# Attention of a macaron block on one core: values in batches of eight, masks in pairs at a batch's end, row maxima transposed at its start

## The chip, the cores and the metric

One core of a Trainium2 chip runs the whole program. Times are device microseconds (us) of one execution; the kernel before took 3117.17 us as the median of three runs (3116.67 to 3117.39). Engines are called PE (TensorE, the matmuls), DVE (VectorE), ACT (ScalarE), POOL (GpSimd) and SP (SyncE, which issues the transfers).

## What is computed

A block of 2048 tokens of 512 features: a feed-forward part, attention, and the same feed-forward part again. The change touches the attention alone, with 16 heads of 32 features:

```python
qkv = jnp.einsum('bsd,ed->bse', x, w_qkv) + b_qkv
scores = jnp.einsum('bhqd,bhkd->bhqk', q, k) / math.sqrt(Hd)
scores = scores + causal[None, None]          # -inf above the diagonal
attn = jax.nn.softmax(scores, axis=-1)
out = jnp.einsum('bhqk,bhkd->bhqd', attn, v)
```

The weights are scaled up, so that scores are large and each row's maximum has to be taken off before the exponential.

## The kernel before

Three stages run in the attention: `project_in` (line 788) makes queries, keys and values, `attention` (line 1125) works through the heads, `project_out` (line 1330) multiplies with the output weights. The change is in `attention`, in the class `Heads` (line 622) that serves it, and in the share of head 0 that `project_in` does at its end.

**Two passes over the scores.** A head's scores are computed twice on PE. The first time, queries stand on the output partitions: 40 chunks a head (`CHUNKS`, `max_chunk`, line 705) of up to 512 columns, of which DVE takes the row maximum (`take_max`, line 729; chunks on the diagonal are masked in the same instruction). When the last chunk of one of the four blocks of 512 queries is reduced, `split_max` (line 748) joins the maxima and splits them in two parts; PE transposes these in `rows` (line 719, four small matmuls with 2 columns of weights), and ACT copies the two rows under the head's queries (`store_rows`, line 761). The second time, keys stand on the output partitions: 40 tiles a head (`TILES`, `scores`, line 1196) of 128 keys by up to 512 queries, with the maximum subtracted by the two extra rows. A tile on the diagonal (16 of 40) gets a second, small bf16 matmul (line 1213, 128 columns) that adds the mask. ACT takes the exponential (`exps`, line 1273), and PE multiplies the result with the values (`with_values`, line 1217): 33 columns of weights, the values and a column of ones whose product is the softmax's sum. `TILES` alternates between two lanes, which write partitions 0 and 64 on, so that two products run side by side. `take_out` (line 1281) copies the output banks, twice a head.

**Banks.** PSUM has 8 banks: 3 for scores, 3 for chunks and transposed rows (`MAX_BANKS`), 2 for outputs. PE may write score tile u when the exponential of u - 3 is done, and an item of the maxima (`ITEMS`) when the item three before is taken out.

**The order.** It is written out by hand. In slot t of 40 of a head (`head`, line 1232), PE issues the score tile t + 4, the chunks of the next head that belong to slot t (one, in slots 0, 9, 18 and 27 two, in the last four none), and, in slots 17, 28, 35 and 39, the transposed rows of blocks 3, 2, 1 and 0 of the next head. After every fourth slot come four products with the values. So there are ten batches of products a head. Two lines set the distances:

```python
BATCH = 4
AHEAD = 4
```

Each engine works through its own list in order, so a wait holds up all that stands behind it on the engine. The last head has no next one, so it has no chunks, and ACT converts the output weights (line 1306) just before it. For head 0, the chunks and rows are spread over the last steps of `project_in` (`head_items_after`, line 778); the last step has nine of the 44 items, rows 1 and rows 0 as its last.

Of the kernel before, what the change touches and what calls it, by code (L numbers as in the profile page):

```python
# [8 lines left out]
F32 = mybir.dt.float32  # L9
# [585 lines left out]
SCORE_BANKS = 3  # L595
BATCH = 4
AHEAD = 4
RING = AHEAD + BATCH


ROWS_AFTER = 4


def chunks_of_slot(t):

    return [m for m in range(SLOTS) if m * (SLOTS - ROWS_AFTER) // SLOTS == t]


MAXED_AT = {[t for t in range(SLOTS) if LAST_CHUNK[b] in chunks_of_slot(t)][0]: b for b in BLOCKS}
ROWS_AT = {t + ROWS_AFTER: b for t, b in MAXED_AT.items()}  # L610

ITEMS = [item for t in range(SLOTS)
         for item in [("chunk", m) for m in chunks_of_slot(t)] + ([("rows", ROWS_AT[t])] if t in ROWS_AT else [])]
MAX_BANKS = 3
DIAGONAL = [m for m in range(SLOTS) if CHUNKS[m][2] == CHUNKS[m][0]]


def max_bank_of(s, item):
    return (len(ITEMS) * s + ITEMS.index(item)) % MAX_BANKS


class Heads:
# [49 lines left out]
    def add_slot(self, nc, ctx):  # L672
        i = len(self.queries)
        self.queries.append(ctx.enter_context(nc.sbuf_tensor(f"queries{i}", [self.ROWS, TOKENS], F32R)))
        self.keys.append(ctx.enter_context(nc.sbuf_tensor(f"keys{i}", [self.ROWS, TOKENS], F32R)))
        self.values.append(ctx.enter_context(nc.sbuf_tensor(f"values{i}", [P, TT, VCOLS], F32)))
        ctx.enter_context(nc.sbuf_tensor(f"values_pad{i}", [P, TT, HD], F32))

# [15 lines left out]
    def wait_for_max_bank(self, pe, hp, s, item):  # L694

        before = len(ITEMS) * s + ITEMS.index(item) - MAX_BANKS
        if before < 0:
            return
        (kind, j), s = ITEMS[before % len(ITEMS)], before // len(ITEMS)
# [18 lines left out]

    def rows(self, pe, hp, s, b):

        pe.wait_ge(self.max_parts_ready, 12 * hp + (4 * s + RANK[b] + 1))
        self.wait_for_max_bank(pe, hp, s, ("rows", b))
# [55 lines left out]
def head_items_after(ep, s, tb):  # L778
# [3 lines left out]
    if i < 0:  # L782
        return []
    end = len(ITEMS) if i == steps - 1 else len(ITEMS) * (i + 1) // (steps + LEFT_TO_LAST)
    return ITEMS[len(ITEMS) * i // (steps + LEFT_TO_LAST):end]

# [338 lines left out]
def attention(nc, bank, o_heads, sums, inverses, w_out, b_out, heads, o):  # L1125
    with ExitStack() as ctx:
# [67 lines left out]
        def _(pe):  # L1194

            def scores(hp, s, t, first=False):

                b, kt = TILES[t]
                i = s % 3
                if t in FIRST_OF_BLOCK:  # L1200
                    pe.wait_ge(heads.rows_ready, 12 * hp + (4 * s + RANK[b] + 1))
                    if s == 2 and t == 0:
                        pe.wait_ge(heads.constants_ready, 9)
                if not (first and t < SCORE_BANKS):
                    pe.wait_ge(probs_ready, 120 * hp + (SLOTS * s + t - SCORE_BANKS + 1))
                q0 = max(b * TB, kt * P)
                width = (b + 1) * TB - q0
                out = score_bank[(SLOTS * s + t) % SCORE_BANKS]
                last = pe.matmul(out[:, 0:width], keys[i][0:ROWS, cols(kt, P)],  # L1209
                                 queries[i][0:ROWS, q0:q0 + width], start=True, stop=(kt < 4 * b),  # L1210
                                 skip_group_check=True)
                if kt >= 4 * b:
                    last = pe.matmul(out[:, 0:P], heads.ident_b[:], heads.key_mask_b[:],
                                     start=False, stop=True, skip_group_check=True)
                last.then_inc(scores_ready, 1)

            def with_values(hp, s, t):
# [4 lines left out]
                if t % BATCH == 0:  # L1222
# [3 lines left out]
                last = pe.matmul(out_bank[BANK_OF[b]][row:row + VCOLS, off:TB], values[i][:, kt, :],  # L1226
                                 probs[:, t % RING, 0:TB - off], start=(t in FIRST_OF_BLOCK),
                                 stop=(t in LAST_OF_BLOCK), skip_group_check=True)
# [3 lines left out]
            def head(hp, s, has_next):  # L1232
                for t in range(SLOTS):
                    if t + AHEAD < SLOTS:
                        scores(hp, s, t + AHEAD)
                    elif has_next:
                        scores(hp, s + 1, t + AHEAD - SLOTS)
                    if has_next:
                        for m in chunks_of_slot(t):
                            heads.max_chunk(pe, hp, s + 1, m)  # L1240
                        if t in ROWS_AT:
                            heads.rows(pe, hp, s + 1, ROWS_AT[t])
                    if t % BATCH == BATCH - 1:
                        for u in range(t + 1 - BATCH, t + 1):
                            with_values(hp, s, u)

            for t in range(AHEAD):
                scores(0, 0, t, first=True)
            with pe.Fori(0, HEADS // 3) as hp:
# [5 lines left out]
        def _(dve):  # L1255
            def head(hp, s):
                for t in range(SLOTS):
                    for m in chunks_of_slot(t):
                        heads.take_max(dve, hp, s + 1, m)
                    if t in MAXED_AT:  # L1260
                        heads.split_max(dve, hp, s + 1, MAXED_AT[t])

# [9 lines left out]
        def _(act):  # L1272
            def exps(hp, s, t):
                b, kt = TILES[t]
                width = TB - max(0, kt * P - b * TB)
                act.wait_ge(scores_ready, 120 * hp + (SLOTS * s + t + 1))
                source = score_bank[(SLOTS * s + t) % SCORE_BANKS][:, 0:width]
                act.activation(probs[:, t % RING, 0:width], source, ACT.Exp, scale=SM_SCALE)\  # L1278
                   .then_inc(probs_ready, 1)

# [6 lines left out]
            def head(hp, s, has_next):  # L1287
                for t in range(SLOTS):
                    if t + AHEAD < SLOTS:
                        exps(hp, s, t + AHEAD)  # L1290
                    elif has_next:
                        exps(hp, s + 1, t + AHEAD - SLOTS)
                    if has_next and t in ROWS_AT:
                        heads.store_rows(act, hp, s + 1, ROWS_AT[t])
                    if t % BATCH == BATCH - 1:
# [3 lines left out]

            for t in range(AHEAD):  # L1300
                exps(0, 0, t)
            with act.Fori(0, HEADS // 3) as hp:
# [233 lines left out]
```

## Time and profile before

| | |
|---|---|
| median of three runs | 3117.17 us |
| the profiled execution, its own time | 3117.0 us |
| its span | 3115.2 us |
| lies around the span | 1.8 us |
| first product with values of head 0, of head 1 | 1296.24, 1337.20 us |
| first product of head 15 | 1892.09 us |
| from one head's first product to the next's, heads 1 to 14 | 39.5 to 39.6 us |
| DMA, mean over the span | 41 GB/s |

Of the span, the feed-forward parts take some four fifths; the heads run from about 1290 to 1922 us. The start of an instruction and its length are given for each; a matmul's length holds a fixed latency besides its streaming, so that neighbours overlap, and what a matmul costs PE is the distance from its start to the start of the next.

### The profile page before, as it was taken

To read this page: it belongs to the slowest core of one execution; us is meant where nothing else is said; L and a number is where in the kernel's file an instruction comes from. 1 tells how busy PE (TensorE), PEld (TensorE's weight loads), DVE (VectorE), ACT (ScalarE), POOL (GpSimd) and SP (SyncE) were. 2 spreads that over 40 slices of the span, in tenths; PEclk is the share of its full clock that TensorE was granted. 3 is DMA by queue.
4 is the path that set the end of the run, shared out by engine and by line. 5 is a ranking of instruction groups with operands and counts; after the bars stand their busy time and mean duration, and the time that the engine had idled before them with its cause. 6 is when DMAs were issued, how large, how long until landed. Compare 5 with 4: busy or idle time off the path is not lost. (4 is left out here: it accounts for less than half of the span.)

```text
span 3115.2 us, 38902 instructions
## 1 busy us (share of the span) xinstructions
PE 2967.1 (95%) x13152; PEld 2206.1 (71%) x13152; DVE 1850.4 (59%) x3290; ACT 1053.0 (34%) x1781; POOL 759.3 (24%) x480
## 2 busy tenths in 40 slices
PE   5999999999999989999999996679999999999999
PEld 3788888888888858644444442458888888888887
DVE  7666655666556574666666662476555665656554
ACT  4322222222222232355555554142222222222222
POOL 4322222222222245200000001343222222222221
PEclk8999999999999989999999998889999999999999
DMA  3000000000000027522222221201000000000001
GB/s 94 21 28 28 24 23 20 27 27 20 27 20 20 1 65 185 149 55 55 55 54 55 54 52 37 88 14 31 24 28 20 25 22 27 27 20 20 27 14 55
DMA packets 120569, 127.58 MB, mean 41 GB/s; under 512 B 72672, under 2 KB 72928, under 8 KB 117152
## 3 DMA queue, kind: packets, MB, share of 16 engines
q1 hardware_dynamic: 119928, 125.93, 15.4%
q8 instruction: 41, 0.67, 0.1%
q10 hardware_dynamic: 552, 0.59, 0.1%
q14 instruction: 48, 0.39, 0.0%
HBM read 96.87 MB, written 29.62 MB: 41 GB/s over the span
## 5 line engine op out<-in xcount | busy, mean ns | idle before, releaser
L61 PE MATMUL psum<-ffn_x_high,ffn_w_high 128*128 128x512 f32 x2048 | 803.6, 392 | 18.6 <-DVE ffn_gelu L389 18.6
L62 PE MATMUL psum<-ffn_x_low,ffn_w_high 128*128 128x512 f32 x2048 | 799.4, 390 | 0.0
L63 PE MATMUL psum<-ffn_x_high,ffn_w_low 128*128 128x512 f32 x2048 | 799.0, 390 | 0.0
L526 POOL TENSOR_TENSOR ffn_inner<-ffn_gelu,ffn_inner 128x512 fp32r<-128x512 f32 x256 | 346.3, 1353 | 1156.3 <-ACT ffn_inner L471 1156.3
L379 DVE SCALAR_TENSOR_TENSOR ffn_gelu<-ffn_gelu,psum 128x512 f32<-128x512 f32 x256 | 176.0, 687 | 599.2 <-ACT ffn_gelu L464 599.1
L61 PEld LDWEIGHTS psum<-ffn_x_high,ffn_w_high 128*128 128x128 f32 x2048 | 386.2, 189 | 104.0 <-DVE ffn_gelu L389 21.9
L62 PEld LDWEIGHTS psum<-ffn_x_low,ffn_w_high 128*128 128x128 f32 x2048 | 386.2, 189 | 82.0 <-issue 2.0
L63 PEld LDWEIGHTS psum<-ffn_x_high,ffn_w_low 128*128 128x128 f32 x2048 | 385.9, 188 | 80.7
L61 PE MATMUL psum<-ffn_inner,ffn_w_high 128*128 128x512 f32 x1024 | 398.6, 389 | 0.2
L62 PE MATMUL psum<-ffn_inner,ffn_w_high 128*128 128x512 f32 x1024 | 398.4, 389 | 0.0
L63 PE MATMUL psum<-ffn_inner,ffn_w_low 128*128 128x512 f32 x1024 | 398.4, 389 | 0.0
L1278 ACT ACTIVATE probs<-psum 128x512 f32<-128x512 f32 (+3 forms) x640 | 302.7, 535 | 244.6 <-PE psum L1209 167.0
L736 DVE TENSOR_REDUCE chunk_max<-psum 128x1 f32<-128x512 f32 x384 | 254.4, 687 | 167.8 <-PE psum L714 167.8
L464 ACT ACTIVATE ffn_gelu<-psum 128x512 f32<-128x512 f32 x256 | 152.8, 597 | 531.0 <-PE psum L63 531.0
L395 DVE SCALAR_TENSOR_TENSOR x<-psum,x 128x512 f32<-128x512 f32 x512 | 321.3, 683 | 16.0 <-PE psum L63 16.0
L520 POOL TENSOR_TENSOR ffn_w_low<-ffn_weight,ffn_w_high 128x1024 fp32r<-128x1024 f32 x96 | 232.1, 2418 | 329.5 <-ACT ffn_w_high L457 329.5
L471 ACT ACTIVATE ffn_inner<-ffn_gelu 128x512 fp32r<-128x512 f32 x256 | 161.9, 632 | 381.1 <-DVE ffn_gelu L389 381.1
L383 DVE SCALAR_TENSOR_TENSOR ffn_gelu<-ffn_gelu,psum 128x512 f32<-128x512 f32 x256 | 176.2, 688 | 180.0 <-ACT ffn_gelu L466 180.0
L1226 PE MATMUL psum<-probs,values 128*33 128x512 f32 (+3 forms) x1280 | 266.9, 538 | 0.0
L714 PE MATMUL psum<-keys,queries 96*128 96x512 f32 (+3 forms) x640 | 251.0, 410 | 14.1 <-DVE chunk_max L736 12.6
L1209 PE MATMUL psum<-queries,keys 98*128 98x512 f32 (+3 forms) x640 | 247.0, 404 | 8.1 <-ACT probs L1278 6.6
L457 ACT ACTIVATE ffn_w_high<-ffn_weight 128x1024 fp32r<-128x1024 f32 x96 | 102.0, 1062 | 402.3 <-DVE ffn_weight L370 402.3
(115 smaller groups left out, 3078.5 us busy)
## 6 DMA issues: line engine op xcount, KB each, us to landing
ffn_words<-packed SPq DMA_DIRECT2D x96, 256.0 KB
ffn_word_scales<-scales SPq DMA_DIRECT2D x96, 256.0 KB
qk_parts<-parts SPq DMA_DIRECT2D x32, 512.0 KB, 4.0
queries<-qk_parts SPq DMA_DIRECT2D x48, 256.0 KB, 4.0
keys<-qk_parts SPq DMA_DIRECT2D x48, 256.0 KB, 6.1
x<-x_in SPq DMA_DIRECT2D x4, 1024.0 KB, 13.8
v_parts<-parts SPq DMA_DIRECT2D x16, 256.0 KB, 4.6
values<-v_parts SPq DMA_DIRECT2D x16, 256.0 KB, 7.7
```

Source lines behind the costliest of these rows:

```text
L61: pe.matmul(out, w_high, x_high, start=first, stop=False, skip_group_check=True)
L62: pe.matmul(out, w_high, x_low, start=False, stop=False, skip_group_check=True)
L63: return pe.matmul(out, w_low, x_high, start=False, stop=last, skip_group_check=True)
L383: dve.scalar_tensor_tensor(out=cubic[m], in0=square[m], scalar=1.0, in1=gate_bank[m], op0=ALU.add, op1=ALU.mult)\
L395: dve.scalar_tensor_tensor(out=x[:, k, cols(tb, TB)], in0=down_bank[k], scalar=FFN_BACK, in1=x[:, k, cols(tb, TB)], op0=ALU.mult, op1=ALU. ...
L520: pool.tensor_tensor(w_low[s][:, :, piece, :], weight[:, q % 2, :, :], f32(w_high[s][:, :, piece, :]), ALU.subtract).then_inc(w_low_ready, 1)
L526: pool.tensor_tensor(inner[:, tb % 2, m, 1, :], product[m], f32(inner[:, tb % 2, m, 0, :]), ALU.subtract)\
L714: last = pe.matmul(out[:, 0:width], self.queries[i][0:self.STACK, cols(qt, P)], self.keys[i][0:self.STACK, c * TB:c * TB + width], start=T ...
L736: dve.tensor_reduce(chunk_max, scores, AX.X, ALU.max).then_inc(self.max_taken, 1)
L1209: last = pe.matmul(out[:, 0:width], keys[i][0:ROWS, cols(kt, P)], queries[i][0:ROWS, q0:q0 + width], start=True, stop=(kt < 4 * b), skip_g ...
L1226: last = pe.matmul(out_bank[BANK_OF[b]][row:row + VCOLS, off:TB], values[i][:, kt, :], probs[:, t % RING, 0:TB - off], start=(t in FIRST_O ...
L1278: act.activation(probs[:, t % RING, 0:width], source, ACT.Exp, scale=SM_SCALE)\
```

## The change

- `BATCH` and `AHEAD` become 8: after every eighth slot come eight products with the values, five batches a head. The ring of probabilities grows from 8 to 24 tiles; the scores run 8 tiles ahead.
- The score tiles of a batch are issued in a new order (`ORDER`): first the unmasked ones of lane 0, then those of lane 1, then the masked ones. The products keep their order. The masks of two neighbouring masked tiles are added together (`masks`), after both tiles' scores and the chunks of both slots.
- Each slot has exactly one chunk.
- Rows are transposed at the beginning of slots 0, 8, 16 and 32, ahead of the slot's score, so right behind a batch of products (slots 0, 8, 16, 32 follow slots 39, 7, 15, 31). Blocks 3 and 2 are still transposed during the head before (slots 16 and 32), blocks 1 and 0 only in the head's own slots 0 and 8. ACT's `store_rows` moves with them.
- In `project_in`, rows 1 and rows 0 are left out, so 42 items are spread. The last step has nine: rows 2 and chunks 32 to 39.

What the new constants come to, by the code. The numbers are score tiles, in the order of issue, eight to a stretch between two batches of products; a star marks a masked tile, with its width:

```
slots  0- 7: tiles  8 12 14  9 13 15 10*(256) 11*(256)          chunks  0- 7, rows 1 first
slots  8-15: tiles 18 20 19 21 16*(384) 17*(384) 22*(512) 23*(512)   chunks  8-15, rows 0 first
slots 16-23: tiles 24 26 28 30 25 27 29 31                      chunks 16-23, rows 3 first
slots 24-31: tiles 32*(512) 33*(512) 34*(384) 35*(384) 36* 37*(256) 38* 39*(128)   chunks 24-31
slots 32-39: tiles  0  2  6  1  3  7  4*(128) 5*(128), next head    chunks 32-39, rows 2 first
```

Tile 33, 35, 37, 39 of lane 1 and 32, 34, 36, 38 of lane 0 have the widths of their pair. The core of the diff:

```diff
-BATCH = 4
-AHEAD = 4
-RING = AHEAD + BATCH
-ROWS_AFTER = 4
+BATCH = 8
+AHEAD = BATCH
+RING = 3 * BATCH
+DIAGONAL_TILES = [t for t in range(SLOTS) if TILES[t][1] >= 4 * TILES[t][0]]
+ORDER = [t for j in range(0, SLOTS, BATCH)
+         for t in sorted(range(j, j + BATCH), key=lambda t: (t in DIAGONAL_TILES, t not in DIAGONAL_TILES and t % 2, t))]
+ROWS_AT = {0: 1, 8: 0, 16: 3, 32: 2}
+OWN_ROWS = (1, 0)
...
-                if kt >= 4 * b:
-                    last = pe.matmul(out[:, 0:P], heads.ident_b[:], heads.key_mask_b[:],
-                                     start=False, stop=True, skip_group_check=True)
-                last.then_inc(scores_ready, 1)
+                if kt < 4 * b:
+                    last.then_inc(scores_ready, 1)
+
+            def masks(s, u):
+                for v in (u - 1, u):
+                    pe.matmul(score_bank_of(s, v)[:, 0:P], heads.ident_b[:], heads.key_mask_b[:],
+                              start=False, stop=True, skip_group_check=True).then_inc(scores_ready, 1)
...
             def head(hp, s, has_next):
                 for t in range(SLOTS):
-                    if t + AHEAD < SLOTS:
-                        scores(hp, s, t + AHEAD)
-                    elif has_next:
-                        scores(hp, s + 1, t + AHEAD - SLOTS)
+                    if t in ROWS_AT and (has_next or ROWS_AT[t] in OWN_ROWS):
+                        heads.rows(pe, hp, s + (ROWS_AT[t] not in OWN_ROWS), ROWS_AT[t],
+                                   alone=not has_next)
+                    of, u = divmod(t + AHEAD, SLOTS)
+                    if has_next or of == 0:
+                        scores(hp, s + of, u)
                     if has_next:
-                        for m in chunks_of_slot(t):
-                            heads.max_chunk(pe, hp, s + 1, m)
-                        if t in ROWS_AT:
-                            heads.rows(pe, hp, s + 1, ROWS_AT[t])
+                        heads.max_chunk(pe, hp, s + 1, t)
+                    if (has_next or of == 0) and ORDER[u] in DIAGONAL_TILES and ORDER[u] % 2 == 1:
+                        masks(s + of, u)
                     if t % BATCH == BATCH - 1:
-                        for u in range(t + 1 - BATCH, t + 1):
-                            with_values(hp, s, u)
+                        for v in range(t + 1 - BATCH, t + 1):
+                            with_values(hp, s, v)
```

ACT's and DVE's loops follow the same order. Two of three pads beside the values go, which makes room for the larger ring.

## Rows read from the trace of the kernel before

**Rows 1.** The page: span, and busy time of each engine.
```profile
span 3115.2 us, 38902 instructions
PE 2967.1 (95%) x13152; PEld 2206.1 (71%) x13152; DVE 1850.4 (59%) x3290; ACT 1053.0 (34%) x1781; POOL 759.3 (24%) x480
```

**Rows 2.** PE, PEld, DVE, ACT, POOL busy, clock, DMA by stretch: heads; one; head 14.
```profile
1296.00:1921.00 625.00, 606.08 (x2996) 289.86 (x2997) 364.31 (x1255) 351.61 (x725) 4.53 (x1) 0.99 0.25 51
...
1376.70:1416.30 39.60, 38.56 (x195) 18.70 (x195) 24.36 (x85) 22.33 (x47) 0.00 (x0) 1.00 0.28 55
1851.40:1892.10 40.70, 37.31 (x190) 17.92 (x189) 23.88 (x83) 23.50 (x47) 0.59 (x1) 1.00 0.04 10
```

**Rows 3.** Waits over ten heads (1416 to 1811 us): us in total, times, longest.
```profile
DVE chunk_max L736 <- PE psum L714: 112.2, 80, 3.7
ACT probs L1278 <- PE psum L1209: 104.6, 60, 2.2
...
PEld psum L714 <- DVE chunk_max L736: 25.6, 60, 1.1
...
PEld psum L1209 <- ACT probs L1278: 8.5, 20, 0.7
```

**Rows 4.** Timeline of PE around a batch of products: start, length, instruction.
```profile
1822.24 0.39 PE L714 MATMUL psum<-keys,queries 96*128 96x512 f32 x1
1822.47 0.39 PE L1209 MATMUL psum<-queries,keys 98*128 98x512 f32 x1
1822.70 0.40 PE L714 MATMUL psum<-keys,queries 96*128 96x512 f32 x1
1823.03 1.91 PE L1226 MATMUL psum<-probs,values 128*33 128x512 f32 x8
1824.87 0.50 PE L1209 MATMUL psum<-queries,keys 98*128 98x512 f32 x1
1825.21 0.23 PE L714 MATMUL psum<-keys,queries 96*128 96x128 f32 x1
```

**Rows 5.** Timeline of PE at a mask, and at a mask ahead of products.
```profile
1821.12 0.23 PE L1213 MATMUL psum<-key_mask_b,ident_b 128*128 128x128 bf16 x1
1821.16 0.48 PE L714 MATMUL psum<-keys,queries 96*128 96x512 f32 x1
1821.48 0.33 PE L1209 MATMUL psum<-queries,keys 98*128 98x384 f32 x1
...
1919.29 0.23 PE L1213 MATMUL psum<-key_mask_b,ident_b 128*128 128x128 bf16 x1
1919.45 1.05 PE L1226 MATMUL psum<-probs,values 128*33 128x512 f32 x4
```

**Rows 6.** Timeline of PE at transposed rows, four matmuls merged.
```profile
1825.79 0.40 PE L724 MATMUL psum<-ident_r,max_parts 128*2 128x128 f32 x4
1826.03 0.45 PE L1209 MATMUL psum<-queries,keys 98*128 98x512 f32 x1
1826.33 0.23 PE L1213 MATMUL psum<-key_mask_b,ident_b 128*128 128x128 bf16 x1
```

**Rows 7.** Exponentials: timeline of ACT, PE's wait on it, and by form.
```profile
1839.36 0.58 ACT L764 ACTIVATE queries<-psum 2x512 fp32r<-2x512 f32 x1
1839.97 1.36 ACT L1278 ACTIVATE probs<-psum 128x512 f32<-128x512 f32 x3
...
1846.78 2.06 ACT L1278 ACTIVATE probs<-psum 128x512 f32<-128x512 f32 x4 [1.47 <-PE psum L1209]
...
1847.43 0.49 PE L1209 MATMUL psum<-queries,keys 98*128 98x512 f32 x1 [0.22 <-ACT probs L1278]
...
L1278 ACT ACTIVATE probs<-psum 128x384 f32<-128x384 f32 x46 | 21.1, 492 | 17.8 <-PE psum L1213 17.3
```

**Rows 8.** Timeline: two row maxima on DVE; PE's longest wait on them.
```profile
1857.16 1.29 DVE L736 TENSOR_REDUCE chunk_max<-psum 128x1 f32<-128x512 f32 x2 [0.94 <-PE psum L714]
...
1835.98 0.38 PE L714 MATMUL psum<-keys,queries 96*128 96x256 f32 x1 [0.82 <-DVE chunk_max L736]
```

**Rows 9.** Timeline of PE: last rows of head 0; the wait before head 15.
```profile
1288.46 0.40 PE L724 MATMUL psum<-ident_r,max_parts 128*2 128x128 f32 x4 [1.21 <-DVE max_parts L758]
...
1891.65 0.50 PE L1209 MATMUL psum<-queries,keys 98*128 98x512 f32 x1 [2.34 <-ACT probs L1278]
```

More of the change, by code:

```diff
@@ L595, with place_of, item_at @@
 SCORE_BANKS = 3
-BATCH = 4
-AHEAD = 4
-RING = AHEAD + BATCH
-ROWS_AFTER = 4
[L604 to L610, printed above, removed]
+BATCH = 8
[4 more added lines that the diff above has]
+         for t in sorted(range(j, j + BATCH), key=lambda t: (t in DIAGONAL_TILES, t not in DIAGONAL_TILES and t % 2, t))]
+FIRST_SCORE = [u for u in range(SLOTS) if TILES[ORDER[u]][0] not in [TILES[t][0] for t in ORDER[:u]]]
+ROWS_AT = {0: 1, 8: 0, 16: 3, 32: 2}
+OWN_ROWS = (1, 0)
 ITEMS = [item for t in range(SLOTS)
-         for item in [("chunk", m) for m in chunks_of_slot(t)] + ([("rows", ROWS_AT[t])] if t in ROWS_AT else [])]
+         for item in ([("rows", ROWS_AT[t])] if t in ROWS_AT else []) + [("chunk", t)]]
+ITEMS_BEFORE = [item for item in ITEMS if item[0] == "chunk" or item[1] not in OWN_ROWS]
 MAX_BANKS = 3
 DIAGONAL = [m for m in range(SLOTS) if CHUNKS[m][2] == CHUNKS[m][0]]
+def place_of(s, item):
+    during = s if item[0] == "rows" and item[1] in OWN_ROWS else s - 1
+    if during < 0:
+        return ITEMS_BEFORE.index(item)
+    return len(ITEMS_BEFORE) + len(ITEMS) * during + ITEMS.index(item)
+def item_at(place):
+    if place < len(ITEMS_BEFORE):
+        return ITEMS_BEFORE[place], 0
+    during, i = divmod(place - len(ITEMS_BEFORE), len(ITEMS))
+    return ITEMS[i], during + (ITEMS[i][0] == "chunk" or ITEMS[i][1] not in OWN_ROWS)
 def max_bank_of(s, item):
-    return (len(ITEMS) * s + ITEMS.index(item)) % MAX_BANKS
+    return place_of(s, item) % MAX_BANKS
 class Heads:
@@ L694, in wait_for_max_bank @@
     def wait_for_max_bank(self, pe, hp, s, item):
-        before = len(ITEMS) * s + ITEMS.index(item) - MAX_BANKS
+        before = place_of(s, item) - MAX_BANKS
         if before < 0:
             return
-        (kind, j), s = ITEMS[before % len(ITEMS)], before // len(ITEMS)
+        (kind, j), s = item_at(before)
         if kind == "chunk":
@@ L1256, in head @@
             def head(hp, s):
[L1257 to L1261, printed above, removed]
+                for m in range(SLOTS):
+                    heads.take_max(dve, hp, s + 1, m)
+                    if m == LAST_CHUNK[CHUNKS[m][0]]:
+                        heads.split_max(dve, hp, s + 1, CHUNKS[m][0])
             heads.fill_ones(dve, 2)
@@ L1272, in _, with exps @@
         def _(act):
-            def exps(hp, s, t):
+            def exps(hp, s, u):
+                t = ORDER[u]
                 b, kt = TILES[t]
                 width = TB - max(0, kt * P - b * TB)
[L1276 to L1279, printed above, removed]
+                act.wait_ge(scores_ready, 120 * hp + (SLOTS * s + u + 1))
+                act.activation(probs[:, (SLOTS * s + t) % RING, 0:width], score_bank[(SLOTS * s + u) % SCORE_BANKS][:, 0:width],
+                               ACT.Exp, scale=SM_SCALE).then_inc(probs_ready, 1)
             def take_out(hp, s, e):
@@ L1288, in head @@
                 for t in range(SLOTS):
[L1289 to L1294, printed above, removed]
+                    if t in ROWS_AT and (has_next or ROWS_AT[t] in OWN_ROWS):
+                        heads.store_rows(act, hp, s + (ROWS_AT[t] not in OWN_ROWS), ROWS_AT[t])
+                    of, u = divmod(t + AHEAD, SLOTS)
+                    if has_next or of == 0:
+                        exps(hp, s + of, u)
                     if t % BATCH == BATCH - 1:
@@ L1298, in head @@
                                 take_out(hp, s, e)
-            for t in range(AHEAD):
-                exps(0, 0, t)
+            for u in range(AHEAD):
+                exps(0, 0, u)
             with act.Fori(0, HEADS // 3) as hp:
```

39 lines of the change are left out of this document (23 added, 16 removed).

## The prediction

> **What bounds the kernel now.** I read the page first: PE is busy for 95% of the span [rows 1]. Then the stretches: over all heads PE is busy for 606 of 625 us, ACT for 352 and DVE for 364, and in one head for 38.6, 22.3 and 24.4 of 39.6 us, at a granted clock of 1.00, the upper level (2.4 GHz) [rows 2]. So a head takes what its matmuls take in a row, and what PE waits. The list of waits says who waits for whom: DVE and ACT wait for PE for over 100 us in ten heads; PE waits for DVE 2.6 us a head and for ACT 0.9 us, counted at the weight loads, where part is hidden under the matmul before [rows 3]. Outside the heads nothing is touched but the last step of head 0's maxima. DMA is no bound.
>
> The timeline then prices PE's own order, start to start. In steady state a score tile or chunk of 512 columns takes 0.23 us [rows 4]. At an edge to the products more goes: from chunk to first product 0.33 (0.10 over 0.23), and four products take 1.84 us to the next score, of which two pairs are twice 0.86, 0.03 the first product's surplus and 0.10 the way back; the first score behind then takes 0.34 (0.10 over) [rows 4]. **One edge pair: 0.32 us.** A mask takes 0.04 us itself, and the chunk behind it 0.32, so 0.08 over: 0.12 us together [rows 5].
>
> **Part 1, batches of eight.** Ten edge pairs a head become five: 5 x 0.32 = 1.6 us less. The products' own time stays.
>
> **Part 2, masks.** Before: 16 x 0.12 = 1.9 us. Four of the eight pairs end a batch, four stand in its middle (one in slots 8-15, three in 24-31). The trace has no two masks in a row. The nearest row is four transposes in a row, 0.24 us for four 128-column matmuls, so 0.06 [rows 6]; a step at 0.10 is my upper bound, from the first surplus of an edge [rows 4]. I take 0.06, as it is of the same width; nothing can undercut the 0.04 that stands behind a mask now [rows 5]. A middle pair then costs 0.06 + 0.04 + 0.08 = 0.18; a pair ahead of the products 0.06 for the first, 0.16 for the second up to the product [rows 5], less the 0.10 that the chunk's own edge would cost: 0.12. Together 4 x 0.18 + 4 x 0.12 = 1.2: **0.7 us less**. The step from a chunk to a mask isn't shown; between 0 and 0.06 over, I take 0, as behind a score.
>
> **Part 3, rows.** Four transposes take 0.24, and the score behind them 0.30, 0.06 over [rows 6]. Before, two groups stand in mid-stream (0.30 each) and two ahead of products (0.24 each): 1.1 us. After, four stand behind products, where the way back is paid anyhow, and the score behind costs 0.06 over in place of 0.10: 4 x 0.20 = 0.8. **0.3 us less**, if the step from products to transposes costs the 0.10 of the way back; its bounds are 0 and 0.17 (0.10 and a second surplus of 0.07), so 0.4 us a head on one side and 0.3 on the other.
> The trace shows that surplus on both sides of every batch, and less of it between transposes and scores [rows 4, 6]. The Trainium skill, TensorEngine Tiling (Array Packing), Key Properties, says that a change of tiling mode drains the engine. Weights of 2 and of 33 columns could be two modes, and then transposes behind products save no edge; that is rival D below.
>
> The three parts make 2.6 us. The surplus of 0.06 also falls on what stands two places behind any narrow matmul (as behind the transposes [rows 6]), and the new order packs narrow tiles and masks together: 0.2 back. **Work on PE: 2.4 us less a head.**
>
> **Part 4, the new waits.** This is what the change pays with. There are still three score banks and three banks for maxima. While PE does eight products (3.6 us), ACT and DVE empty three banks each (1.5 to 2 us) and then idle; in the scoring stretch behind they must follow PE at once.
> - ACT: exponentials of 512 start every 0.48 us ((2.06 - 0.62)/3) and take 0.60; PE's waiting score starts 0.65 after the exponential's start [rows 7]. PE's slot is 0.47, so ACT just keeps up if it begins in time. But copying rows takes ACT 0.61 to the next exponential [rows 7], and it now stands at the front of four stretches, at slots 0 and 32 behind a take-out besides. The first exponential then starts 0.8 to 1.1 us behind its score instead of 0.5, and the fourth score waits: about 0.29, 0.36, 0.17 and 0.07 us; the scores behind it some 0.35 more. That is 1.2.
> - Masks: a masked tile's exponential can start only behind the mask, which now comes 0.5 us later. In a run of pairs, mask at T; exponential at T + 0.27; it is done at T + 0.87 for 512 columns (0.60), and the bank is free at T + 0.92. PE has 0.06 + 0.04 + 0.26 + 0.23 = 0.59 us of work until it wants that bank: waits 0.33. For 384 columns (0.49 [rows 7]) 0.28 in the middle run and 0.16 in slots 8-15, for 256 about 0.17. That is 0.9.
> - DVE: a maximum of 512 starts every 0.61 us, slower than PE's slot of 0.47, and frees its bank 0.75 behind its start [rows 8]. Chunk 7 of a stretch wants the bank of chunk 4: 0.43 + 4 x 0.61 + 0.75 = 3.62 us behind the first, PE is there after 3.3; diagonal chunks shorten both, the joining of maxima adds 0.7 to DVE. Slots 24-31 and 32-39 come out at 0.37 and 0.41, the rest below 0.2. Against that the doubled slot 27 goes, whose second chunk waited 1.23 us from start to start, 1.0 over its 0.23 [rows 8]: 1.0 after, where 1.4 was.
> All waits together: 3.1 us a head, where 1.8 is now (chunks 1.4, exponentials 0.4). **1.3 us more.** And behind a wait the next matmul takes 0.10 more, as behind any break: the score that waited 0.22 has 0.49 for its length where a steady one has 0.39 [rows 4, 7]. Some 15 such places against 6: **0.9 us more.**
>
> Sum a head: -2.44 + 1.28 + 0.88 = -0.28 us. The same chain of sums for the kernel before gives 39.4 us a head where the trace has 39.5, so I trust it to a few tenths.
>
> **Part 5, the ends.** Heads 1 to 14: 14 x -0.28 = -3.9 us. Head 14's end and head 15: the conversion of the output weights on ACT makes PE wait 2.34 us [rows 9]; it stays, since ACT's next exponential again stands behind it. Head 15 has no chunks, so it gains its edges and masks (-2.3) but ACT sets the pace of five of eight scores, and two groups of rows come in (0.4): -1.3 in all. In the last step for head 0, PE waits 1.21 us for the last maxima [rows 9], then ACT copies the rows. Both last groups leave, chunk 32 comes in with 0.61 on DVE: -0.5. DMAs, SP's queue and POOL keep their order; a head's queries and keys are first wanted by its chunks, a head ahead of its scores, as before.
>
> **Sum:** -3.9 - 1.3 - 0.5 = -5.7 us. The profiled execution took 3117.0 us (span 3115.2), the median is 3117.17: forecast **3111.5 us**. A measurement of this kernel can tell about 0.2%, 6.2 us, from no change: so the forecast lies just within "same", and faster begins at 3110.9.
>
> **Rivals.**
> A, *the waits don't grow.* If PE's waits for ACT and for DVE mostly fall together or are hidden, only half of the 2.2 us of part 4 comes: -1.3 a head, 15 heads -20 us and 0.5 at the start, 3097. For it: at one place PE can wait for one only; before, PE waited little [rows 3]. Against: ACT's pace (0.48) and DVE's (0.61) are both above PE's slot. Chance 0.14.
> C, *slower: ACT loses step in every stretch.* Once the first exponential is 0.5 us late, PE's slot (0.47) never lets ACT (0.48) catch up, so that nearly each of the five scores behind the third bank in five stretches waits a little and pays 0.10 behind it: 23 such places in place of my 15, 0.8 us more a head, so +0.5 a head against before, 15 x 0.5 = +8 us: 3125. It decides once the waits and what follows them exceed 4.9 us a head (my sum has 3.1 and 1.5). For it: rows at the front of four stretches [rows 7]. Chance 0.16.
> D, *the new edges cost the upper bound* (products to transposes +0.07, mask to mask 0.10): 0.3 + 0.3 = 0.6 us a head, +9 us on the forecast: 3120. By the rule on tiling modes the first half of it comes, and 3116. Chance 0.16.
> E, *it doesn't do what it says:* masks end only four of eight pairs; that is counted. No chance of its own.
>
> **How the numbers follow.** My case 0.54, of which 0.24 falls below 3110.9 and 0.30 above; A 0.14; C 0.16; D 0.16. Faster: 0.24 + 0.14 = 0.38. Slower (over 3123.4): most of C and a small part of D, 0.17. Same: 0.45. The range holds my case (3103 to 3120), D, the nearer half of A and most of C: 3098 to 3125. The likeliest case's own range is 3103 to 3120.
>
> **What would show it.** From one head's first product to the next's 39.2 us (39.5 now). Five batches of 3.6 us at full width, 0.16 from mask to product, two masks 0.06 apart. PE's waits for exponentials about 2.2 us a head, in the fourth score of the stretches and in the second score behind masks; waits for maxima about 0.9, at chunks 31 and 39. Wrong if the waits stay below 2 us a head (then A), or if PE loses over 0.10 at each of the new edges (D).

## The result, and the profile after

The changed kernel takes 3137.98 us (median of four runs, 3136.82 to 3140.63), the kernel before 3116.92 beside it (four runs, 3115.24 to 3117.39): a ratio of 1.0071 (1.0058 to 1.0083). It is slower by 21 us, and lies outside the range.

The page of the changed kernel, to be held against [rows 1]: the span has grown by 20.9 us, PE's busy time by 16.8, though PE has the same 13152 matmuls.
```profile
span 3136.1 us, 38873 instructions
PE 2983.9 (95%) x13152; PEld 2215.1 (71%) x13152; DVE 1844.1 (59%) x3290; ACT 1047.4 (33%) x1781; POOL 759.0 (24%) x480
```

More busy time with the same matmuls points to a slower PE. The stretches from a head's first product to the next's show it (columns as in [rows 2]): head 1, head 7 and head 14 of the changed kernel.
```profile
1340.93:1380.24 39.31, 38.17 (x195) 18.80 (x194) 24.09 (x86) 21.84 (x46) 0.00 (x0) 1.00 0.27 52
...
1584.21:1625.13 40.92, 39.79 (x195) 19.22 (x193) 24.12 (x86) 21.84 (x46) 0.00 (x0) 0.96 0.25 49
...
1870.86:1913.65 42.79, 39.00 (x187) 18.06 (x185) 22.07 (x78) 23.64 (x48) 3.80 (x1) 0.95 0.03 9
```
Head 1 has a clock of 1.00 and takes 39.31 us, 0.24 less than the 39.55 that heads 1 to 13 take on average before (514.2 us for thirteen). Head 7 has the same instructions and a granted clock of 0.96. Heads 3 to 13 are all of the second kind (40.9 to 41.0 us). Cut finer around the end of head 7's scores, in pieces as long as what stands out there:
```profile
1612.80:1616.20 3.40, 2.82 (x12) 1.68 (x11) 3.01 (x16) 3.08 (x7) 0.00 (x0) 1.00 0.16 40
1616.20:1619.60 3.40, 3.40 (x11) 1.11 (x13) 1.97 (x11) 0.45 (x2) 0.00 (x0) 0.50 0.00 0
1619.60:1623.00 3.40, 3.28 (x24) 1.93 (x20) 1.44 (x3) 2.22 (x5) 0.00 (x0) 1.00 0.08 20
```
The granted clock is at its upper level (2.4 GHz), falls to 0.50 (1.2 GHz) for 3.4 us and is back at 1.00. In that time PE, busy throughout, gets done what takes about 1.7 us at full clock (an estimate, half the length). PE's timeline shows what it did before and what was hit:
```profile
1612.63 0.40 PE L1228 MATMUL psum<-queries,keys 98*128 98x512 f32 x1
1612.89 0.49 PE L728 MATMUL psum<-keys,queries 96*128 96x512 f32 x1
...
1613.60 0.47 PE L1228 MATMUL psum<-queries,keys 98*128 98x512 f32 x1 [0.22 <-ACT probs L1302]
...
1615.47 0.33 PE L1228 MATMUL psum<-queries,keys 98*128 98x128 f32 x1
1616.16 0.78 PE L728 MATMUL psum<-keys,queries 96*128 96x512 f32 x1 [0.36 <-DVE chunk_max L761]
...
1616.74 0.44 PE L1236 MATMUL psum<-key_mask_b,ident_b 128*128 128x128 bf16 x2
1617.11 3.14 PE L1248 MATMUL psum<-probs,values 128*33 128x512 f32 x10
```
The fall comes just behind slots 32 to 39, where PE waits for ACT at the fourth score and for DVE at chunk 39 (0.69 from the score's start to the chunk's). Chunk 39 takes 0.78 instead of 0.40, and the first pairs of products start about 0.85 apart instead of 0.43. Heads 1 and 2 of the same kernel have the same thin stretch, and no fall. Of head 1:
```profile
1369.50:1372.90 3.40, 2.82 (x13) 1.66 (x11) 3.01 (x16) 3.10 (x7) 0.00 (x0) 1.00 0.16 40
```
There are twelve falls, one a head in heads 3 to 14, and they recur every 40.96 us, which is the length of a head with a fall.

**Where the 20 us are.** Up to the last product (1921.53 before, 1941.81 after):
- Heads 1 to 13: 529.9 us against 514.2, so +15.75. That is 13 x -0.24 = -3.1, eleven falls at 40.95 - 39.31 = 1.64, together +18.0, and 0.87 in head 2, which has no fall (40.18 us); its cause is below. (Heads 5, 8 and 11 would have that 0.87 too; the fall covers it there, so it adds only some 0.7 to these three.)
- Head 14: 42.79 against 40.72 (the time before is 39.5 to 39.6 only for heads 1 to 13), +2.1, with the twelfth fall. (Both kernels have one more fall at the beginning of head 15, behind PE's wait for the conversion of the output weights.)
- The start: head 0's first product 1296.24 before and 1300.52 after, head 1's 1337.20 and 1340.93, so +3.7. Of this, 2.5 is only place: the first product now stands eight tiles and three chunks later in the order (11 x 0.23), and heads 14 and 15 have that much less. The first score itself comes earlier, 1289.20 against 1290.07. The rest, about 2 us, fits the clock, as follows.
- Head 15: 28.16 against 29.44, -1.3, though its eight tiles less make 1.8 by themselves.

At the start, DVE and ACT hold PE up in both kernels, and the clock falls in both. Of the kernel before, at the fall and at the return:
```profile
1288.00:1289.00 1.00, 0.40 (x4) 0.21 (x4) 0.33 (x2) 0.11 (x1) 0.00 (x0) 0.94 0.46 98
...
1299.00:1300.00 1.00, 1.00 (x6) 0.47 (x3) 0.00 (x0) 0.00 (x0) 0.00 (x0) 0.94 1.45 163
```
Of the changed kernel:
```profile
1285.00:1286.00 1.00, 0.72 (x2) 0.43 (x2) 0.96 (x5) 0.00 (x0) 0.00 (x0) 0.55 0.29 113
...
1302.00:1303.00 1.00, 1.00 (x6) 0.23 (x4) 0.00 (x0) 0.00 (x0) 0.00 (x0) 0.91 0.17 43
```
So the low clock lasts from 1288.9 to 1299.1 before, and from 1285.1 to 1302.2 after. From the first score on that is 9.0 and 13.0 us, and four more microseconds at half rate would cost two. No run took this apart.

**The order itself ran as forecast.** Timeline of PE in head 7, slots 24 to 31, of the changed kernel:
```profile
1603.51 0.40 PE L728 MATMUL psum<-keys,queries 96*128 96x512 f32 x1
1603.75 0.29 PE L1236 MATMUL psum<-key_mask_b,ident_b 128*128 128x128 bf16 x2
1603.85 0.42 PE L1228 MATMUL psum<-queries,keys 98*128 98x384 f32 x1
1604.11 0.40 PE L728 MATMUL psum<-keys,queries 96*128 96x512 f32 x1
1604.67 0.44 PE L1228 MATMUL psum<-queries,keys 98*128 98x384 f32 x1 [0.16 <-ACT probs L1302]
...
1607.68 0.29 PE L1236 MATMUL psum<-key_mask_b,ident_b 128*128 128x128 bf16 x2
1607.89 1.48 PE L1248 MATMUL psum<-probs,values 128*33 128x512 f32 x6
```
Two masks take 0.29 together where one takes 0.23 [rows 5]: a step of 0.06 to 0.07. Behind a pair comes the wait for ACT that part 4 has (1604.67, 0.56 behind the start ahead of it). From the first mask to the first product are 0.21, so 0.15 from the second. The step from products to transposes was 0.52 from start to start, which is 0.10 over the 0.42 of a product behind a product, the value I took; the score behind the four transposes stands 0.06 over.

The waits over ten heads (1416 to 1811 us, as in [rows 3]):
```profile
DVE chunk_max L753 <- PE psum L728: 121.7, 48, 3.8
ACT probs L1302 <- PE psum L1236: 72.6, 77, 3.9
ACT heads_out L1309 <- PE psum L1248: 58.0, 18, 3.3
...
PEld psum L1228 <- ACT probs L1302: 46.4, 173, 0.5
...
PEld psum L728 <- DVE chunk_max L753: 4.0, 13, 0.7
```
PE's weight loads wait for exponentials 4.6 us a head, where they waited 0.9 before, and for DVE 0.9 us a head (0.4 of it at this line) where they waited 2.6: the bound between matmuls has gone from DVE to ACT, as part 4 says, though part of these loads' waits is hidden under the matmul before. From start to start, over the steady step, I estimate PE's waits in head 1 at 1.9 us for exponentials and 1.0 for maxima, where the prediction has 2.2 and 0.9. ACT's side of it: the take-out at 1611.63, the rows, and then six exponentials without a gap.
```profile
1611.63 0.60 ACT L1309 ACTIVATE heads_out<-psum 97x512 f32<-97x512 f32 x1 [3.24 <-PE psum L1248]
1612.25 0.58 ACT L781 ACTIVATE queries<-psum 2x512 fp32r<-2x512 f32 x1
1612.86 3.04 ACT L1302 ACTIVATE probs<-psum 128x512 f32<-128x512 f32 x6
```

### The profile page after: what moved, and what is told of

The parts are those of the page before. It is cut to its first block and busy times, and to the rows that moved or that the text cites. A ratio compares the mean times of both kernels' runs of the same rounds, so it can differ in the third digit from the quotient of the medians.

```text
span 3136.1 us, 38873 instructions
## 1 busy us (share of the span) xinstructions
PE 2983.9 (95%) x13152; PEld 2215.1 (71%) x13152; DVE 1844.1 (59%) x3290; ACT 1047.4 (33%) x1781; POOL 759.0 (24%) x480
## 5 line engine op out<-in xcount | busy, mean ns | idle before, releaser
L61 PEld LDWEIGHTS psum<-ffn_x_high,ffn_w_high 128*128 128x128 f32 x2048 | 386.2, 189 | 102.8 <-DVE ffn_gelu L389 20.9
L753 DVE TENSOR_REDUCE chunk_max<-psum 128x1 f32<-128x512 f32 x384 | 247.8, 684 | 189.1 <-PE psum L728 188.9
L1302 ACT ACTIVATE probs<-psum 128x512 f32<-128x512 f32 (+3 forms) x640 | 293.7, 544 | 121.6 <-PE psum L1236 116.0
L1228 PE MATMUL psum<-queries,keys 98*128 98x512 f32 (+3 forms) x640 | 268.9, 426 | 16.2 <-ACT probs L1302 10.3
L728 PE MATMUL psum<-keys,queries 96*128 96x512 f32 (+3 forms) x640 | 241.6, 383 | 10.2 <-DVE chunk_max L761 5.7
```

Of the source, the lines that this page charges most:

```text
L61: pe.matmul(out, w_high, x_high, start=first, stop=False, skip_group_check=True)
L728: last = pe.matmul(out[:, 0:width], self.queries[i][0:self.STACK, cols(qt, P)], self.keys[i][0:self.STACK, c * TB:c * TB + width], start=T ...
L753: dve.tensor_reduce(chunk_max, scores, AX.X, ALU.max).then_inc(self.max_taken, 1)
L1228: last = pe.matmul(score_bank_of(s, u)[:, 0:width], keys[i][0:ROWS, cols(kt, P)], queries[i][0:ROWS, q0:q0 + width], start=True, stop=(kt ...
L1302: act.activation(probs[:, (SLOTS * s + t) % RING, 0:width], score_bank[(SLOTS * s + u) % SCORE_BANKS][:, 0:width], ACT.Exp, scale=SM_SCALE ...
```

## The experiments

Every ratio is to the kernel before, run beside it on the same chip (medians 3115.8 to 3116.0). My theory: the new waits thin out PE's work in slots 32 to 39, and the clock answers. The rival: what falls is tied to something else in the order (the pairs of masks, the long row of products), or the time is in the waits themselves.

**1. Fill the waits.** The changed kernel with five matmuls a head more. Each writes a score's bank just before the score itself does, so nothing of it is left.
```diff
+                for _ in range({2: 2, 7: 1, 34: 1, 36: 1}.get(u, 0)):
+                    pe.matmul(score_bank_of(s, u)[:, 0:TB], keys[i][0:ROWS, cols(kt, P)],
+                              queries[i][0:ROWS, cols(b, TB)], start=True, stop=True, skip_group_check=True)
```


> The changed kernel, with five extra matmuls a head whose results are overwritten: a full-width score tile into a tile's own bank just ahead of the real one (two ahead of tile 2 of the order, one ahead of tiles 7, 34 and 36). They stand where PE waits right behind for an exponential or a maximum, so most of their 0.24 us each is hidden. Nothing else changes. Theory 1 (the loss is the clock: PE idles so much in slots 32 to 39 that the granted clock falls to 1.2 GHz for 3.4 us in every head from the fifth on, 1.6 us each): the falls vanish or become rare, a head takes 39.4 to 39.7 us in place of 40.9, the whole 3116 to 3122. Theory 2 (the waits and new edges themselves cost it, the lower clock comes from something else, as the masks in pairs or the time since the last fall): the falls stay at one a head, a head takes 40.9 to 41.5 us, the whole 3137 to 3145.

Measured: 3124.22 us (eight runs), 1.0025 (1.0015 to 1.0036). With more work it is 14 us faster than the changed kernel, though 2 us above what was expected. Head 7, and the piece of it that ends with the scores of slots 32 to 39:
```profile
1581.03:1620.39 39.36, 38.91 (x200) 19.70 (x198) 24.14 (x86) 21.85 (x46) 0.00 (x0) 1.00 0.26 51
...
1609.60:1613.00 3.40, 3.27 (x15) 2.03 (x13) 3.00 (x16) 3.13 (x7) 0.00 (x0) 1.00 0.16 40
```
PE is busy 3.27 of 3.40 us where it was 2.82, and no head from 1 to 13 has a fall. ACT and DVE have the same work, so it is neither the pairs of masks nor the row of products as such. Nine heads take 39.3 to 39.4 us, but heads 2, 5, 8 and 11 take 40.12 to 40.20, at a clock of 1.00. That is head 2 of the changed kernel again, where the falls had hidden it elsewhere.

**What every third head has** is DVE's loop, which runs over three heads and jumps back behind chunk 39. DVE in the kernel before, then in experiment 1:
```profile
1410.65 0.16 DVE L758 TENSOR_TENSOR max_parts<-minus_max,max_parts 128x4 fp32r<-128x4 f32 x1
1414.49 0.69 DVE L736 TENSOR_REDUCE chunk_max<-psum 128x1 f32<-128x512 f32 x1 [3.68 <-PE psum L714]
```
```profile
1535.37 0.17 DVE L775 TENSOR_TENSOR max_parts<-minus_max,max_parts 128x4 fp32r<-128x4 f32 x1
1538.39 1.29 DVE L753 TENSOR_REDUCE chunk_max<-psum 128x1 f32<-128x512 f32 x2 [2.85 <-PE psum L728]
```
And PE's timeline in experiment 1:
```profile
1536.74 0.39 PE L728 MATMUL psum<-keys,queries 96*128 96x512 f32 x1
...
1538.21 0.51 PE L1231 MATMUL psum<-queries,keys 98*128 98x512 f32 x1
...
1539.14 0.33 PE L728 MATMUL psum<-keys,queries 96*128 96x128 f32 x1 [0.42 <-DVE chunk_max L753]
```
The chunk is issued at 1536.74 and done at about 1537.13, but DVE begins with it at 1538.39: it has stood still for 2.85 us behind its last instruction of the head. Before, the chunk itself came only at 1413.98, 3.2 us behind DVE's last instruction, as slots 36 to 39 had none. So the jump lay under a gap, which one chunk in every slot closes. The Trainium skill, Runtime: NRT & Kernel Launch, Instruction fetch mechanics, says that branching breaks the sequential prefetch; these 2.85 us are in line with that, and the page has no figure.

**2. The same filling elsewhere.** As many matmuls, most of them in other slots.
```diff
+                for _ in range(0 if first else {10: 2, 22: 1, 26: 1, 36: 1}.get(u, 0)):
```


> The changed kernel with five overwritten full-width matmuls a head as in e_fill, but none in slots 32 to 39 (two ahead of tile 10, one each ahead of tiles 22, 26 and 36 of the order; none in the first head). Theory 1 (the clock falls where slots 32 to 39 are thin): the falls stay, eight or more of 16 heads, 40.9 us each, the whole 3130 to 3140. Rival (any extra matmuls in the head, anywhere, keep the clock up): no falls, 3116 to 3124.

Measured: 3136.91 us (four runs), 1.0068 (1.0051 to 1.0084). Heads 1 to 5 take 39.3 and 39.4 (40.1 and 40.4 with the jump); from head 6 on each has a fall. Head 7, the piece before its fall, and the fall:
```profile
1582.16:1623.11 40.95, 40.08 (x199) 20.16 (x198) 24.16 (x86) 21.84 (x46) 0.00 (x0) 0.96 0.26 49
...
1610.80:1614.20 3.40, 2.82 (x12) 1.72 (x11) 3.01 (x16) 3.05 (x7) 0.00 (x0) 1.00 0.16 40
1614.20:1617.60 3.40, 3.40 (x11) 1.04 (x13) 1.90 (x11) 0.45 (x2) 0.00 (x0) 0.53 0.00 0
```
So more work in the head doesn't keep the clock up by itself; work in the thin stretch does. Here the stretch has 2.82 us of 3.40 again. Heads 1 to 5 have it too, though, at a clock of 1.00.

**3. Shift the head's length.** Three overwritten matmuls where PE doesn't wait, to see whether the recurrence needs a head of just this length.
```diff
+                for _ in range(0 if first else {19: 1, 25: 1, 29: 1}.get(u, 0)):
```


> The changed kernel with three overwritten full-width matmuls a head (ahead of tiles 19, 25 and 29 of the order) in places where PE doesn't wait, so none is hidden: 0.5 to 0.7 us a head more, 39.9 us without a fall of the clock and 41.5 with one. In the changed kernel the falls come 40.96 us apart, which is just the length of a head with a fall, so each meets the next head at the same place. Theory (a thin stretch is only followed by a fall if it comes at the right time, and the falls repeat because the head's length fits): fewer falls, 3 to 7, so the kernel gets faster although work is added: 3125 to 3133. Rival (the fall depends on the thin stretch alone, whenever it comes): a fall in 12 heads, 3144 to 3148.

Measured: 3133.57 us (four runs, 3125.62 to 3143.39), 1.0062 (1.0040 to 1.0083). In the profiled execution heads take 39.5 us, so three matmuls of 0.23 added only 0.2, and one head from 1 to 13 has a fall (41.13). The stretch is as thin as ever. Of head 7:
```profile
1609.70:1613.10 3.40, 2.82 (x13) 1.66 (x11) 3.01 (x16) 3.11 (x7) 0.00 (x0) 1.00 0.16 40
```
So the rival is out (3144 to 3148, a fall in every head): the thin stretch alone doesn't make a fall. The theory's 3125 to 3133 is just missed. But the runs lie 18 us apart, and their mean clock (0.970 in the slowest, 0.977 in the two fastest) says that others have more falls. Moving the head by 0.2 us makes the falls fewer and irregular; what makes one happen isn't settled by it.

**4. Masks right behind their own tile.** The changed kernel without the pairs (`masks` and its two calls go).
```diff
-                if kt < 4 * b:
-                    last.then_inc(scores_ready, 1)
+                if kt >= 4 * b:
+                    last = pe.matmul(score_bank_of(s, u)[:, 0:P], heads.ident_b[:], heads.key_mask_b[:],
+                                     start=False, stop=True, skip_group_check=True)
+                last.then_inc(scores_ready, 1)
```


> The changed kernel with each mask right behind its own score tile, as before the change; batches of eight, the order of tiles and the rows stay. The sums say: four waits of the second tile of a pair (0.9 us a head) and the edges behind them go, single masks cost 0.5 more: 38.6 us a head where the clock stays up. PE's idle time in slots 32 to 39 is nearly as long as in the changed kernel. Theory 1 (clock): falls come where a head's thin stretch meets them, but a head without a fall is 38.6 us, so the falls don't repeat at every head: some 3 to 8 of 16 heads, the whole 3104 to 3113. Theory 2 (masks in pairs cause the fall): no fall at all in the heads, 3103. If the batches of eight themselves cost the time: 3130 or more.

Measured: 3123.77 us (eight runs, 3120.07 to 3136.92), 1.003 (1.0018 to 1.0043). Head 7:
```profile
1581.87:1620.77 38.90, 37.56 (x194) 18.82 (x193) 24.11 (x86) 21.85 (x48) 0.00 (x0) 1.00 0.27 54
```
A head without fall or jump takes 38.9 us, 0.4 less than with the pairs. There are falls only at two places, one of 6.8 us across heads 5 and 6 (41.21 and 40.91 us) and one in head 11 (40.50), both in the heads with the jump. The whole is above the 3104 to 3113 expected: the head has 38.9 where 38.6 was forecast, and every third head has the jump besides.

**5. And the tiles in their plain order.** As 4, with
```diff
+ORDER = list(range(SLOTS))
```


> As e_inline, and tiles also in their plain order: only the batches of eight, the one chunk a slot and the rows at a batch's start remain. The sums say 39.0 us a head without a fall of the clock (the second score tile of the next head, of block 2, now stands one slot behind the rows and waits 0.7 us for them). Theory 1: 3110 to 3118 with a few falls, 3110 with none. Theory 2 (order of tiles makes no difference): as e_inline within 2 us.

Measured: 3125.05 us (ten runs), 1.0029 (1.0019 to 1.0039). That is above the 3110 to 3118 expected. Heads without fall or jump take 39.06 to 39.22; falls come at the end of heads 5 and 11 again and reach into the next heads (39.58 and 40.03). What is left of the change here is batches of eight, rows at their beginning and one chunk a slot: together 0.4 below the 39.55 of before. The order of the tiles is worth another 0.2 (38.9), and the pairs of masks take 0.4 back (39.31).

**6. The pairs alone**, in the kernel before.
```diff
+            def masks(s, t):
+                if TILES[t][1] >= 4 * TILES[t][0] and t % 2 == 1:
+                    for v in (t - 1, t):
+                        pe.matmul(score_bank[(SLOTS * s + v) % SCORE_BANKS][:, 0:P], heads.ident_b[:],
...
+                        masks(s + (t + AHEAD) // SLOTS, (t + AHEAD) % SLOTS)
```


> The kernel before with one part of the change alone: masks two by two behind the second tile's slot, batches of four. The sums say that the masks' own cost falls by 0.4 us a head and waits for exponentials rise from 0.4 to 1.2, chunk edges and rows the rest: 40.6 us a head in place of 39.5, so 3117 + 15 x 1.1 = 3132 to 3136, with the clock up throughout, since no stretch gets thinner than before. Rival (pairs of masks are cheap, the waits for them hidden by the products that follow at once): 3108 to 3117.

Measured: 3134.77 us (four runs), 1.0059 (1.0042 to 1.0076). Head 7, and PE's waits for exponentials over ten heads:
```profile
1583.07:1623.83 40.76, 39.28 (x194) 18.92 (x193) 24.57 (x85) 22.44 (x47) 0.00 (x0) 1.00 0.26 52
```
```profile
PEld psum L1209 <- ACT probs L1285: 37.9, 70, 0.8
```
There is no fall in heads 1 to 14, and yet the heads up to 13 take 40.66 to 40.79, 1.2 us more, as expected. PE's loads wait for ACT 3.8 us a head, where it was 0.9. So pairs of masks cost more in waits than they save in matmuls, more in batches of four than in the new order.

**7. The rows alone**, in the kernel before: right behind products.
```diff
-ROWS_AT = {t + ROWS_AFTER: b for t, b in MAXED_AT.items()}
+ROWS_AT = {16: 3, 28: 2, 32: 1, 36: 0}
```


> The kernel before with one part of the change alone: rows transposed at the start of slots 16, 28, 32 and 36, right behind four products, in place of the ends of slots 17, 28, 35 and 39; batches of four. My term for this part: 0.3 us a head less on PE, so 39.2 us a head and 3112 if no wait comes in its place. Rival (PE comes to rows 1 and rows 0 before DVE has joined the maxima, and ACT's copy stands at the front of four slots): waits of 0.3 us or more a head, 3116 to 3122.

Measured: 3124.48 us (ten runs), 1.0027 (1.0017 to 1.0037); heads take 39.9 to 40.0, 0.4 more, without a fall: above both expectations. PE and then ACT behind the rows:
```profile
1613.21 0.40 PE L724 MATMUL psum<-ident_r,max_parts 128*2 128x128 f32 x4
1613.45 0.91 PE L1209 MATMUL psum<-queries,keys 98*128 98x512 f32 x3
...
1614.91 0.50 PE L1209 MATMUL psum<-queries,keys 98*128 98x512 f32 x1 [0.55 <-ACT probs L1278]
```
```profile
1613.65 0.58 ACT L764 ACTIVATE queries<-psum 2x512 fp32r<-2x512 f32 x1 [1.97 <-PE psum L724]
```
The copy stands ahead of the first exponential, and the fourth score pays for it, as part 4 has it. What the transposes save is less than all that this order costs.

**8. Filling, and the jump moved.** As 1, without filling in the first head, and DVE's loop turned so that it jumps behind chunk 31.
```diff
-                    heads.take_max(dve, hp, s + 1, m)
...
+            TURN = 32
...
+            with dve.Fori(0, HEADS // 3 - 1) as hp:
+                for s in range(1, 4):
+                    maxima(hp, s, range(TURN, SLOTS))
+                    maxima(hp, s + 1, range(TURN))
```


> e_fill with two alterations: no extra matmuls in the first head, and DVE's loop turned, so that its jump back stands behind chunk 31, ahead of a full batch of products, and no longer at the head's end. In the traces DVE stands still for 2.8 us at its jump, every third head; in e_fill that makes PE wait 0.8 us, in the kernel before four slots without chunks cover it. Theory (DVE's jump): the heads 2, 5, 8, 11 and 14 fall from 40.2 to 39.4 us, 4 us in all, and the first head some 2 us: 3117 to 3120. Rival (every third head is longer for PE's or ACT's jump, or for the store and load of heads): 40.2 stays, 3122 to 3124.

Measured: 3121.9 us (ten runs), 1.0022 (1.0012 to 1.0032). The long heads move with the loop, from 2, 5, 8 and 11 to 3, 6 and 9, which shows that the jump makes them. They are 0.6 over (39.93) where it was 0.8, so the jump is only partly covered there, and the turned loop jumps back three times and not four. Head 6 has a fall besides (41.62). The theory's 39.4 for these heads, and its 3117 to 3120, were not reached.

**9. All that helped.** Masks behind their own tile, the loop turned, and one matmul of filling each at tiles 2, 7, 37 and 38.

> What the runs so far point to: batches of eight and rows at a batch's start, each mask right behind its tile, DVE's loop turned, and four overwritten matmuls a head in waits (tiles 2, 7, 37, 38). Heads of 38.9 us without falls and without long third ones: 14 x (38.9 - 39.6) = -10 us, start +4, end -1: 3107 to 3111, faster than before. If the masks' order isn't what counts, 39.3 us a head and 3113 to 3117.

Measured: 3113.25 us (ten runs), 0.9989 (0.9979 to 0.9998). That is above the 3107 to 3111 expected, and in the 3113 to 3117 of the other case, though the heads have the 38.9 of the first. No head from 1 to 13 has a fall; head 7:
```profile
1578.30:1617.15 38.85, 38.14 (x198) 19.37 (x197) 24.11 (x86) 22.01 (x48) 0.00 (x0) 1.00 0.27 52
```
Heads 3, 6 and 9 take 39.5. Heads 1 to 13 gain 7.2 us on the kernel before (1850.71 - 1343.76 against 514.2), but head 1's first product comes at 1343.76, 6.6 us later than there, of which 2.5 is place: more than half of the gain is lost at the start.

**10. The same with one pair left,** `PAIRED = (22, 23)`, the last two tiles of their batch, whose masks stand ahead of products.

> e_best with one pair of masks, the one in which my sums see a gain: tiles 22 and 23, the last of their batch, whose masks are added together behind both slots' chunks. 0.1 us a head less than e_best by the sums: 3110 to 3113, e_best's 3113.3 at the least. If pairs of masks cost more than single ones in every place: 0.2 us a head more, 3115 to 3118.

Measured: 3112.59 us (eleven runs), 0.9987 (0.9978 to 0.9996); heads take 38.8 (39.4 with the jump), 0.1 less than in experiment 9, as the sums had it; between the two runs' times no difference is clear. It beats both kernels, but the kernel before by 0.13% only, which is less than the 0.2% named in the prediction.

## Why the prediction was wrong

- **The term for the steady head was right in its sum,** in part by luck (see part 2 below). It said -0.28 us; a head without a fall has -0.24. Steps between masks (0.06), to transposes (0.10 over) and back were as taken, and the waits stood where it put them: second tile behind masks (0.45 to 0.56 from start to start), fourth score (0.71 in slots 32 to 39), chunks 31 (0.46) and 39 (0.69).
- **The step that failed is the clock it took for given:** "at a granted clock of 1.00" is read from [rows 2] and then kept in every sum of parts 4 and 5. The new waits change it. Forecast for heads 1 to 14: -3.9; measured +17.8, of which some 19.7 are twelve falls at 1.64. Experiment 1 shows that work put into the thin stretch ends the falls, experiment 2 that the same work elsewhere does not, and experiment 3 that the thin stretch isn't enough for a fall.
- **PE's busy time alone doesn't tell when the clock falls.** In each head of the kernel before, at the doubled slot 27, there is a stretch with less of it than in the new thin one, behind one wait of 0.8 us, and the clock stays at 1.00 [rows 8]. Of its head 7:
```profile
1595.30:1598.70 3.40, 2.59 (x12) 1.44 (x8) 1.87 (x9) 2.06 (x4) 0.00 (x0) 1.00 0.00 0
```
  So the thin stretch is where the falls come, and filling it ends them, but why this one is hit and that one not is open.
- A warning was in the kernel before. The two waits of [rows 9] were read for their length only, and the clock falls behind both: for 10.2 us at the start of head 0, and at that of head 15, of which a stretch of the kernel before shows:
```profile
1894.00:1898.00 4.00, 4.00 (x17) 1.80 (x15) 0.00 (x0) 1.64 (x4) 2.04 (x1) 0.69 0.00 0
```
  The prediction took the clock from stretches of a whole head, where it reads 1.00; over all heads [rows 2] has 0.99.
- **"DMAs, SP's queue and POOL keep their order"** left out DVE's own loop. Its jump takes 2.85 us and was covered by the four slots without a chunk, which part 4 only counted as a gain (the doubled slot). Uncovered, it costs 0.8 in a head without a fall; in the changed kernel that is seen in head 2, and in heads 5, 8 and 11 the fall hides it.
- **The start**, -0.5: the first score comes 0.87 earlier, so the step was right; but the clock is low for four microseconds more from there on, which would take 2 us back. Head 15, -1.3: less the tiles that are only displaced, it is +0.6.
- **Part 2** counts the pairs as a gain of 0.7 a head on PE; with their waits in part 4 (0.9) and 0.10 behind each of four, its own terms make +0.6. Measured is +0.4 (39.31 against 38.9 in experiment 4), so the pairs were a loss by the prediction's own sum, and weren't told as one. All the rest then had -0.9; measured are -0.4 for batches, rows and chunks and -0.2 for the order of the tiles, for which the prediction had no term of its own. The two errors, -0.2 and +0.3, nearly cancel. No run has the batches of eight without the rows and the chunks, so part 1 isn't confirmed by itself, and part 3 alone lost 0.4 a head in batches of four (experiment 7).
- **The rivals.** A is out: the waits for exponentials grew (0.9 to 4.6 us a head at the weight loads). C had the side and, with 3125, the nearest number, but not the mechanism: heads at full clock don't take the 40.0 us it says. D's edges didn't come: the step to transposes is 0.10 over and not 0.17, that between masks 0.06 to 0.07.
- **Open:** why heads 1 and 2 have the same waits and no fall; what the chip weighs, and when. The recurrence at the length of a head suggests that falls and heads lock together once they fit, since experiment 2 goes from none to one in every head at head 6. Where a head with a fall has another length, the fall doesn't come again in the next one: 41.13 us in experiment 3, 41.62 in experiment 8. That is in line with it, but no run was made to show it. Why the low clock at the start lasts longer wasn't tried by itself either.

## What to carry to other kernels

Where PE is the bound at the full clock, a cluster of waits can cost more than its length, as the clock may fall behind it: look at the granted clock in pieces of a few microseconds, around the waits that the kernel before already has, ahead of summing anything. If a cluster can't be avoided, a few matmuls whose result is overwritten can be cheaper than the gap. And before an order is made even, ask what each gap in it covered: here it was a loop's jump on another engine.

## What the runs showed of the hardware

- PE's granted clock fell to 0.50 for 3.4 us behind a stretch of 3.40 us in which PE was busy for 2.82, with no gap between matmuls' starts over 0.71 us; with 3.27 in the same place it stayed at 1.00. It also stayed at 1.00 behind stretches of 2.82 in heads 1 and 2 and in experiment 3, and of 2.59 in the kernel before, so this is no rule. The Trainium skill, TensorE: Matmul & The Clock Gate, Why this matters for your kernels, warns of long idle gaps between bursts of matmuls. Keeping to that isn't enough by this trace: the clock fell without such a gap, and the measurement decides.
- At the start of head 0 the clock was low for 10.2 us before and 17.1 after, and it stayed low while PE was busy without a break (1.00 of each microsecond) from 1292 to 1299 before, and from 1294 to 1302 after.
- DVE stood still for 2.80 to 2.85 us at its loop's jump (experiment 1, four jumps), and turning the loop by eight chunks moved PE's longer heads with it.
- With masks behind their own tiles and a clock at 1.00, falls came only in heads with the jump (experiments 4 and 5), so the two costs of this change can also meet: the wait of 2.85 us on DVE may be what sets the clock off there. This was not tried by itself.
